# One decoder layer on one core: quarter sums ahead of the inverse's second level, the output projection begun on the first channels, and the last rows kept in SBUF

## The reference

```python
x = _layernorm(x + _L0_attn_ref(x, ...))        # Hyena: long convolutions
x = _layernorm(x + _L0_xattn_ref(x, ctx, ...))  # cross attention, 64 keys, 16 heads
x = _layernorm(x + _L0_ffn_ref(x, ...))         # gated MLP, 1024 wide, quantized

# Hyena
res = depthwise_conv3(transpose(u @ w_in.T + b_in))
x, v = res[:, :-1], res[:, -1]
h = hyena_filter(...)                           # two filters for each channel
for n in range(2):
    y = irfft(rfft(v, n=2048) * rfft(h[n], n=2048), n=2048)[..., :L]
    v = y * x[:, n]
return transpose(v) @ w_out.T + b_out
```

## Time and profile before

| | |
|---|---|
| median of three runs | 783.12 us |
| the profiled execution | 786.31 us |
| its span, first to last instruction | 784.5 us |
| mean granted TensorE clock | 0.961 |
| TensorE busy | 694.4 us (89% of the span) |
| VectorE busy | 645.7 us (82%) |
| ACT busy | 376.7 us (48%) |
| GpSimd busy | 366.7 us (47%) |

### The profile page before, as it was taken

How to read it: one execution, slowest core, us unless ns; L and a number is a source line. 1 busy time by engine, 2 the same in 40 slices (tenths; PEclk the granted TensorE clock), 3 DMA queues, 4 the chain that set the end, 5 groups by cost and what they waited for, 6 DMA issues and landing times. The chain is left out here.

```text
span 784.5 us, 12534 instructions
## 1 busy us (share of the span) xinstructions
PE 694.4 (89%) x4414; PEld 507.8 (65%) x4414; DVE 645.7 (82%) x1228; ACT 376.7 (48%) x698; POOL 366.7 (47%) x502
## 2 busy tenths in 40 slices
PE   6889998977998797989778898877999999999996
PEld 2478755865757676567666685446777777555664
DVE  3998778899878999698997875135899997899997
ACT  6332354201272401655012624465666666777886
POOL 0734424744146652167531750262463113787886
PEclk9999999989999899999899999987999999999999
DMA  9430055251053340323911157660000000001103
GB/s 310 116 75 1 1 134 134 54 39 15 1 95 67 121 94 1 61 46 87 140 56 55 33 139 151 231 199 1 2 2 3 3 2 1 1 2 42 42 29 109
DMA packets 37611, 52.81 MB, mean 67 GB/s; under 512 B 4809, under 2 KB 31690, under 8 KB 37292
## 3 DMA queue, kind: packets, MB, share of 16 engines
q0 software_dynamic: 7680, 16.77, 14.1%
q1 hardware_dynamic: 29004, 34.44, 13.0%
q10 hardware_dynamic: 864, 0.79, 0.5%
HBM read 31.04 MB, written 8.39 MB: 50 GB/s over the span
## 5 line engine op out<-in xcount | busy, mean ns | idle before, releaser
L659 ACT ACTIVATE yb<-banks 128x256 f32<-128x256 f32 x64 | 24.4, 385 | 230.1 <-PE banks L412 171.3
L403 PE MATMUL banks<-inv_m,spec_y 128*128 128x256 f32 x384 | 87.6, 381 | 8.0 <-POOL spec_y L780 8.0
L435 PE MATMUL banks<-xt_in,w_in 128*128 128x512 f32 x192 | 86.0, 604 | 1.4 <-DMA w_in<-in_w_in_t 1.4
L403 PEld LDWEIGHTS banks<-inv_m,spec_y 128*128 128x128 f32 x384 | 72.3, 190 | 20.7 <-POOL spec_y L780 11.2
L360 PE MATMUL banks<-z_cplx,fwd_m 128*128 128x256 f32 x240 | 73.0, 386 | 10.5 <-DVE prod L1004 7.5
L779 POOL TENSOR_TENSOR spec_y<-prod 128x256 f32<-128x256 f32 x64 | 49.3, 770 | 64.0 <-DVE prod L1004 63.0
L361 PE MATMUL banks<-z_cplx,fwd_m 128*128 128x256 f32 x240 | 72.3, 383 | 0.0
L435 PEld LDWEIGHTS banks<-xt_in,w_in 128*128 128x128 f32 x192 | 37.0, 194 | 46.5 <-issue 43.3
L374 PE MATMUL banks<-z,fwd_m 128*128 128x256 f32 x168 | 46.0, 436 | 20.9 <-DVE sums_c L951 16.1
L360 PEld LDWEIGHTS banks<-z_cplx,fwd_m 128*128 128x128 f32 x240 | 45.5, 192 | 19.4 <-issue 9.7
L374 PEld LDWEIGHTS banks<-z,fwd_m 128*128 128x128 f32 x168 | 36.4, 222 | 31.6 <-issue 20.5
(11 more groups left out here) (246 smaller groups left out, 1713.7 us busy)
## 6 DMA issues: line engine op xcount, KB each, us to landing
x_tok<-in_x SPq DMA_DIRECT2D x8, 512.0 KB, 4.3
x_tok<-in_b_out POOLq DMA_DIRECT2D x8, 512.0 KB, 12.8
x_scratch<-x_tok SPq DMA_DIRECT2D x8, 512.0 KB, 2.9
x<-x_scratch SPq DMA_DIRECT2D x8, 512.0 KB, 8.8
v_t<-left POOLq DMA_DIRECT2D x8, 511.5 KB, 5.5
x_t<-left POOLq DMA_DIRECT2D x8, 511.5 KB, 4.7
xt_in<-in_x_t SPq DMA_DIRECT2D x3, 1024.0 KB, 6.6
spec_h<-x_scratch SPq DMA_DIRECT2D x6, 512.0 KB, 4.6
```

What stands on the lines that cost most here:

```text
L403: last = mm(bank[:, odd * 2 * P:(odd + 1) * 2 * P], spec_y[:, j + odd, part * D + h * P:part * D + (h + 1) * P], inv_m[:, o:o + 2 * P], st ...
L435: last = mm(proj_pair(b, t)[:, c * 512:(c + 1) * 512], w_in[:, k, TILES[t] * P:(TILES[t] + 1) * P], xt_in[:, k, c * 512:(c + 1) * 512], st ...
```

## The change

1. `quarter_sums` is cut in two. `sums_of_quarters` makes all six sums, the two that need POOL's `s13` among them; `turned_parts` makes the turned parts and the groups' inputs behind them.
2. For sequences 0 to 2 `level_one` of the second convolution's first half writes `ef` and `rot` to the buffers `prod`, for which it waits until POOL has read the last products. So the sums of the next input are made right behind its first part, ahead of its last four rotations, of `level_two` (which takes the memory of `left` for its steps) and of the turned parts.
3. `out_project` begins with the first product of four of the eight token tiles as soon as POOL's gate is there (`gated` at 4b + 3), and waits for VectorE's only behind them.
4. The last sequence's rows stay in SBUF (`x_toks`, `row_sum`, now made outside both blocks). Their squares move to ACT's start in the attention block, their factors and their norm to POOL (`norm_last`), which writes them straight to `x2`. The filter block neither stores nor loads them.
5. `Q_EARLY` is 5: chunk 5 is turned and multiplied in the attention block. Chunk 4's queries come ahead of the last output projection. In the attention block, the values are made in two pairs around the scores of tile 0, and the chunks 5, 6 and 7 are turned and multiplied in tiles 0, 1 and 2, in the two banks `ps_ctx` and `ps_inv`. VectorE evacuates the values instead of ACT, and the exponential's table is loaded at ACT's start.
6. The weight sums are made in six halves in tiles 3 to 8, their total in tile 10; POOL norms chunk 0 before it rounds the first weights.

```diff
-def hyena(nc, d, x1_dram, fwd_m, w_in, ident, xt_in, x1_even, left, ld_kv):
+def hyena(nc, d, x1_dram, fwd_m, w_in, ident, xt_in, x1_even, left, x_toks, row_sum, ld_kv):
...
-            out_groups(B - 1, True)
-            sp.wait_ge(st_x1, 16 * GROUPS * B)
+            sp.wait_ge(st_x1, 16 * GROUPS * (B - 1))
...
-                pe.wait_ge(gated, 4 * (b + 1))
+                def out_tile(i, half, dt):
+                    t0 = (2 * i + half) * P
+                    return mm(FB[i][:, half * D:(half + 1) * D], v_t[:, dt, t0:t0 + P], w_out[:, dt, :],
+                              start=(dt == 0), stop=(dt == DT - 1))
+
+                pe.wait_ge(gated, 4 * b + 3)
                 for i in range(L // P // 2):
                     if i % 2 == 0:
                         pe.wait_ge(prod_done, multiplied - 2 + i)
...
+                    out_tile(i, 0, 0)
+                pe.wait_ge(gated, 4 * (b + 1))
+                for i in range(L // P // 2):
+                    out_tile(i, 0, 1)
+                    out_tile(i, 1, 0)
+                    out_tile(i, 1, 1).then_inc(out_mm, 1)
...
-            turn_rows(5, FB[2:4])
+            queries(4, IB[0:2], [(first_level, 4 * (4 * B - 1) + n + 1) for n in range(2)])
             pe.wait_ge(query_evac, DT * 4)
-            pe.wait_ge(rows_evac, DT * 6)
             out_project(B - 1, 8 * 2 * B)
-            queries(4, IB[0:2], [(first_level, 4 * (4 * B - 1) + n + 1) for n in range(2)])
-            queries(5, IB[2:4], [(first_level, 4 * (4 * B - 1) + n + 3) for n in range(2)])
...
-            evac_rows(5, FB[2:4])
-            squares(B - 1)
-            norm(B - 1)
             evac_queries(4, IB[0:2])
-            evac_queries(5, IB[2:4])
...
                 stt(r5[:, 0], r2[:, 1], -ROOT_HALF, x0, ALU.mult, ALU.add).then_inc(x_read, 1)
-                signal(tt(turned_c[:, 0, 0], r2[:, 0, hi], r2[:, 1, hi], ALU.subtract))
-                signal(tt(turned_c[:, 0, 1], r2[:, 0, hi], r2[:, 1, hi], ALU.add))
-                dve.wait_ge(vec_seq, seq.now())
-                split(0, 0, r2, ROOT_HALF)
                 dve.wait_ge(s13_ready, s + 1)
                 signal(stt(r1[:, 1], s13[:], ROOT_HALF, x2, ALU.mult, ALU.add))
                 stt(r5[:, 1], s13[:], -ROOT_HALF, x2, ALU.mult, ALU.add).then_inc(x_read, 1)
+
+            def turned_parts(s):
...
+                signal(tt(turned_c[:, 0, 0], r2[:, 0, hi], r2[:, 1, hi], ALU.subtract))
+                signal(tt(turned_c[:, 0, 1], r2[:, 0, hi], r2[:, 1, hi], ALU.add))
...
+                dve.wait_ge(vec_seq, seq.now() - 2)
+                split(0, 0, r2, ROOT_HALF)
...
                 turned_sums(u + 1)
+                turned_parts(u + 1 + ORDER)
                 products(u + 1, 1, right_of=None if last_one else b + 1)
-                quarters_out(u + 1, 0)
-                if not last_one:
+                if last_one:
+                    quarters_out(u + 1, 0)
+                else:
+                    level_one(u + 1, 0, (ef_in_prod, rot_in_prod))
                     turned_sums(u + 2)
+                    dve.wait_ge(*convolved(b + 1, T_X0 - 1))
+                    dve.wait_ge(*convolved(b + 1, T_X0))
+                    level_one_rest(rot_in_prod)
+                    level_two(u + 1, 0, tmp=past_left, at=(ef_in_prod, rot_in_prod))
+                    turned_parts(u + 2 + ORDER)
                     products(u + 2, 0, 0, 4)
...
-Q_EARLY = CHUNKS - CHUNKS_B
+Q_EARLY = CHUNKS - CHUNKS_B - 1
+X_ROWS = CHUNKS - CHUNKS_B
...
+W_TILE = 10
...
+            pe.wait_ge(set_up, 2)
+            make_values(0, 2)
             scores(0)
+            make_values(2, B)
+            turn_x(Q_EARLY)
             for j in range(TILES_ALL):
                 if j + 1 < TILES_ALL:
                     scores(j + 1)
+                if j == 0:
+                    queries(Q_EARLY)
+                if j == 2:
+                    turn_x(Q_EARLY + 2)
                 turn_prob(j)
+                if j == 0:
+                    turn_x(Q_EARLY + 1)
+                if j in (1, 2):
+                    queries(Q_EARLY + j)
...
+            squares_last(0)
+            squares_last(1)
...
             for j in range(TILES_ALL):
                 exponentials(j)
+                if j < 2:
+                    evac_x(Q_EARLY + j)
+                if j == 0:
+                    evac_q(Q_EARLY)
+                if j == 2:
+                    evac_q(Q_EARLY + 1)
+                    evac_x(Q_EARLY + 2)
                 evac_prob(j)
+                if j == 2:
+                    evac_q(Q_EARLY + 2)
...
-                if j in (1, 3):
-                    weight_sum(j // 2 + 1)
+                if j - 3 in range(6):
+                    weight_sum((j - 3) // 2, (j - 3) % 2)
...
+            norm_chunk(0)
             pool.wait_ge(w_scaled, 1)
-            for i, dst in enumerate((w_gate, w_up, w_down)):
-                quantize(i, dst)
-                if i < 2:
-                    norm_chunk(i)
+            quantize(0, w_gate)
+            norm_chunk(1)
+            quantize(1, w_up)
+            quantize(2, w_down)
```

More of the change, by code:

```diff
@@ L456, in out_project @@
                         pe.wait_ge(prod_done, multiplied - 2 + i)
-                    for half in range(2):
-                        t0 = (2 * i + half) * P
-                        o = FB[i][:, half * D:(half + 1) * D]
-                        for dt in range(DT):
-                            last = mm(o, v_t[:, dt, t0:t0 + P], w_out[:, dt, :], start=(dt == 0), stop=(dt == DT - 1))
-                    last.then_inc(out_mm, 1)
+                    out_tile(i, 0, 0)
[4 more added lines that the diff above has]
+                    out_tile(i, 1, 1).then_inc(out_mm, 1)
             pe.wait_ge(ld_net, 16 * 2)
@@ L1278, in attention_and_feed_forward, with late_order @@
         ps_last = [ps_score[:, n * 512:(n + 1) * 512].bitcast(BF16)[:, 0:HALF] for n in range(2)]
+        late_banks = (ps_ctx, ps_inv)
+        def late_order(c):
+            return range(DT)[::-1] if c == CHUNKS - 1 else range(DT)
         score_banks = ps_score[:].rearrange("p (r n) -> p r n", n=512)
@@ L1290, in load_x2 @@
                     .then_inc(ld_x2[c], 16)
-            for c in (*range(Q_EARLY, CHUNKS), 0):
+            for c in (*range(Q_EARLY, X_ROWS), 0):
                 load_x2(c)
@@ L1367, in scores @@
                     pe.wait_ge(shifted, j)
+                else:
+                    pe.wait_ge(k_ready, DT)
+                if j == W_TILE:
+                    pe.wait_ge(w_sums, 6)
+                    mm(score_banks[:, 0, DT * P:DT * P + 6], ones[:], w_sum[:].rearrange("p i h -> p (i h)"), start=True, stop=True)\
+                        .then_inc(w_total, 1)
                 b = j * P // L
@@ L1379, in turn_prob @@
                     pe.wait_ge(pt_evac, j)
+                else:
+                    pe.wait_ge(v_ready, 2 * B)
                 for h in range(PAIRS):
@@ L1382, in turn_prob @@
                 last.then_inc(pt_mm, 1)
-            def weight_totals(i):
-                pe.wait_ge(inv_evac, i)
-                pe.wait_ge(w_sums, 3)
-                mm(ps_inv[:, 504:507], ones[:], w_sum[:], start=True, stop=True).then_inc(w_total, 1)
-                pe.wait_ge(w_floor, 1)
             def sums(i):
                 pe.wait_ge(pt_evac, 2 * i + 2)
-                pe.wait_ge(inv_evac, i) if i else pe.wait_ge(k_evac, DT)
+                pe.wait_ge(inv_evac, i) if i else pe.wait_ge(q_evac, DT * (CHUNKS - Q_EARLY) - 1)
                 for r in range(STRIPS):
@@ L1411, in values @@
                     pe.wait_ge(added, i)
+                else:
+                    pe.wait_ge(q_evac, DT * (CHUNKS - Q_EARLY))
                 b = 2 * i * P // L
@@ L1588, in squares @@
                     c, k = j // CH, j % CH
[L1589 to L1590 removed]
+                    act.wait_ge(squared, j) if j else act.wait_ge(l_squared, 2 * CH)
                     if c >= 2:
@@ L1670, in _, with norm_last @@
             nc.gpsimd.memset(half_neg[:], -0.5).then_inc(set_up, 1)
+            def norm_last(g):
+                pool.wait_ge(l_squared, CH * (g + 1))
+                ts(l_rstd[:, g], l_var[:, g], 1.0 / D ** 3, LN_EPS, ALU.mult, ALU.add).then_inc(l_floored, 1)
+                ts(l_mean[:, g], x_last_sum[:, g], -1.0 / D, 1.0, ALU.mult, ALU.mult).then_inc(l_centred, 1)
+                pool.wait_ge(l_floored, g + 1)
+                tt(l_rstd[:, g], l_rstd[:, g], half_neg[:], ALU.pow).then_inc(l_raised, 1)
+                pool.wait_ge(l_centred, g + 1)
+                pool.wait_ge(l_raised, g + 1)
+                tt(l_shift[:, g], l_rstd[:, g], l_mean[:, g], ALU.mult).then_inc(l_shift_ready, 1)
+                pool.wait_ge(l_shift_ready, g + 1)
+                for k in range(CH):
+                    last = ts(x2[:, (X_ROWS + g) * CH + k, :], x_last[:, g, k, :], l_rstd[:, g, k:k + 1], l_shift[:, g, k:k + 1],
+                              ALU.mult, ALU.add)
+                last.then_inc(l_scaled, 1)
```

(6 more changed lines are left out.)

208 lines of the change are left out of this document (107 added, 101 removed).

## The result

The changed kernel takes 755.87 us (755.24 to 757.25, 4 runs) beside 784.42 us of the kernel before; the ratio is 0.964 with a 95% interval of 0.961 to 0.967. Forecast were 757 us. One execution of the kernel before (1785 us) and one of the kernel with VectorE's gate (1400 us), both far outside the others, are left out of the medians. The profiled execution has a span of 753.4 us, 31.1 us shorter than before, and a mean granted clock of 0.980.

The account below looks back on a forecast made before the run. TensorE and VectorE take turns in the filter stage; TensorE's chain bounds the loop from tile 10. Terms 3.8 + 0 + 8.2 + 10.2 + 4.4 = 26.6 us off the 783.12 us median give about 757 us, range 748 to 768.

Parts of the forecast that it names:

- Part 1: First-to-second convolution passes: PSUM operations run unheld beside GpSimd's real sums; about 0.95 us in each of four, 3.8 us.
- Part 2: Quarter sums ahead of the second level, sequences 0 to 2: 4.2 us freed but given back, mostly to GpSimd's holds; 0 us.
- Rival A: GpSimd's gate doesn't hold VectorE's turned parts: 6.6 us more gained, 750 us; chance 0.13.
- Part 3: Output projection begun on the first channels: idle filled, clock stays; 3.1 + 3.1 + 2.0 = 8.2 us.
- Part 4: End of the filter block: work removed, projection 6.9 us, attention starts at 489.2 instead of 499.40; 10.2 us, bounds 8 and 11.5.
- Part 5: Attention's entry to tile 10: idle of first tiles filled, 66.9 us become 62.7; 4.4 us taken.
- The term for the weight sums and scales: Waits before tile 10: four weight-sum halves delay TensorE's turn, 4.4 us, and the scales 1.1 us.
- the other 57.2 us: TensorE's own work from attention's start to tile 10: keys, values, three chunks and the tiles, without waits.
- Rival B: ACT bounds attention's first tiles: 5.4 us for three chunks, 2.2 us more for weight halves, 764 us; chance 0.22.
- Rivals C and D: C: filter block ends by something else, 762 us, chance 0.13; D: low clock stays in attention's loop, 800 us, chance 0.04.
- the block change: From the filter block's last residual to attention's start: some 0.8 us.

Follow-up runs that it names:

- kernel with VectorE's gate: Changed kernel, sequences 0 to 2, gate of the first channels made by VectorE ahead of its turned parts instead of by GpSimd: 760.49 us, ratio to before 0.970.
- the moved gate: Changed kernel, sequences 0 to 2, GpSimd's gate of the first channels behind its first four additions, bias loads behind the last four: 761.01 us.
- the moved sums: Changed kernel with each half weight sum issued behind ACT's exponential of the same tile, tiles 3 to 8: 752.33 us, ratio to before 0.958.
- part 1 alone: Kernel before with all six quarter sums ahead of the turned parts, nothing reordered around the second level: 775.17 us, ratio 0.987.

## Why the prediction was right, by its steps

**Part 1 (3.8 forecast, 3.3 and alone 3.7, each with 0.7 us of a missing clock fall).** The mechanism held: PSUM operations pass, and one held row is left. Each pass was given 0.95 us and has 0.7, 0.9 and 1.2 in sequences 0 to 2; in the last one it loses 0.2 us in the changed kernel's first profile and gains 0.8 in its second, at a clock of 1.00 in both.

**Part 2 (0, and 0.7).** Worked through for sequence 1, the first turned operation was to pass and the second to wait for the gate's end, and it does so (261.98 to 264.54). Rival A, no hold, would have shown 6.6 us and falls with it, and with the moved gate, where 2.1 us appear at just this place.

**Part 3 (8.2, and 9.2).** The three projections were forecast with 3.1 us each and have 3.1 to 3.7, at clock 1.00 behind 0.90 us of idle. Right, but the price was put down as if the fall came each time; the kernels without early products show it in 10 of 13. The third was to keep 2.0 us, since VectorE is next in the last sequence, and keeps 2.4 (3.4 less 1.0; in the second profile the loss is 0.5): TensorE's wait for VectorE's gate has grown from 3.08 to 3.75 us.

**Part 4 (10.2, and 10.7 or 8.2).** The projection takes 7.07 us (6.9 forecast) and attention starts 1.14 us behind TensorE's last instruction, 0.3 us behind the last residual (0.8 forecast). But 2.4 us of the old length were chance, so the better value is 8.2 to 8.3, just inside the lower bound of 8. No run has part 4 alone; its value is read from stretches.

**Part 5 (4.4, and 6.4 or 5.7).** The order gives what was said and more: 60.5 us instead of 62.7. The term for the weight sums and scales, 5.5 us, is measured as 4.65 (pairs of 9.22, 9.10 and 11.35 us against 8.34), of which the moved sums recover 4.0; the other 57.2 us are measured as 55.9. Against the second profile of the kernel before, which reaches tile 10 after 66.14 instead of 66.86 us, the part gives 5.7 us. Rival B, ACT as the bound of the first tiles, would show TensorE's gaps; there are 0.49, 0.34 and 0.21 us. Rivals C and D did not come: the block change takes 1.14 us, and the loop is at 1.00 from tile 0 on.

**The sum.** 26.6 us were forecast. The five parts have 30.3 us in the first profiles, 27.9 without the chance in part 4, of which 1.3 us are lost again behind tile 10. The second profiles of both kernels are 27.4 us apart, and the medians 28.6 (784.42 to 755.87). The mis-sized terms are part 5 (+1.3 to +2.0), part 3 (+1.0) and, with the better value, part 4 (-1.9). That they cancel is luck; that the sum comes within 2 us is owed to it in part. Still open are the 1.3 us (1.0 in the second profiles) that the changed kernel loses behind tile 10, of which 0.8 us lie behind TensorE's last product in the first profile, and why part 1 alone is 10 us faster by the median. Its profile explains it stretch by stretch, and its four executions have a mean granted clock of 0.969 to 0.973, where those of the kernel before have 0.955 to 0.968, so it isn't one execution's chance; why an edit of VectorE's order keeps TensorE's clock up was not tried.

## What to carry to other kernels

A short wait of TensorE can cost more than its length (here 1.7 us on top of 2.6): ask of each idle what the clock does behind it, and fill it with work whose input is ready, even a quarter of it. An operation held by GpSimd waits for GpSimd's end, whatever its own size, so moving such a hold to a smaller operation gained nothing here (2.1 us gained, 2.15 lost). A load that an engine issues holds up the work behind it in its stream when it must wait (10.90 us here). Put filler work on ACT behind the operation that others wait for, not ahead of it.

## What was not expected of the hardware

A clock fall made a pass faster: 16.2 us against 18.0, since a later GpSimd let VectorE pass first. And the falls are mostly reproducible: two executions of the kernel before have them in the same places with stretches equal within 0.1 us from 35 to 462 us, and yet an edit elsewhere moves them. The Trainium skill, TensorE: Matmul & The Clock Gate, section "Part 1: The HAM clock gate", says that the number of slow matmuls varies between runs of one kernel; that is seen here in the filters' pass, at the end of the filter block, ahead of the last sequence's second pass (a clock of 0.86 and 0.93 in two executions of the changed kernel) and in attention's first four tiles (18.0 and 16.8 us in two of the kernel before). A difference of 1.7 us in one stretch should therefore be checked against a second execution before it is given to an edit.
